# A megakernel of two decoder layers: many-head attention with scores made by query and by key, and no turned probabilities

## What is computed

```python
x = x + _L0_attn_ref(_layernorm(x), qk, ov)                  # one head, causal
x = x + _L0_xattn_ref(_layernorm(x), ctx, ctx, mask, ...)    # 16 heads of 16, masked
x = x + _L0_ffn_ref(_layernorm(x), ...)                      # top 4 of 16 blocks
x = x + _L1_attn_ref(_layernorm(x), ...)                     # 16 heads, no mask
x = x + _L1_xattn_ref(_layernorm(x), ctx, ctx, tokens, ...)  # 16 heads, rotary, masked
x = x + _L1_ffn_ref(_layernorm(x), ...)                      # 2 of 8 experts, and shared
```

```python
scores = jnp.einsum('bqhd,bkhd->bhqk', qh, kh) * scale       # masked where the stage says so
probs = jax.nn.softmax(scores, axis=-1)
out = jnp.einsum('bhqk,bkhd->bqhd', probs, vh)
```

## Time and profile before

| | us |
|---|---|
| median of 3 runs | 775.46 (774.58 to 775.52) |
| span of the profiled execution | 771.1 |
| S1, from its first scores | 136.62 |
| S3 | 147.21 |
| S4 | 160.77 |

### The profile page before, as it was taken

The page is one execution under the profiler, slowest core; times in us unless marked ns, Lnnn a source line. Parts: engine busy times, 40 slices in busy tenths (PEclk is TensorE's granted clock), DMA queues, the critical chain, the costliest instruction groups (busy, mean ns, idle before and its releaser), DMA issues.

```text
span 771.1 us, 16963 instructions
## 1 busy us (share of the span) xinstructions
PE 743.9 (96%) x5960; PEld 608.3 (79%) x5960; DVE 540.9 (70%) x1461; ACT 415.1 (54%) x1236; POOL 332.9 (43%) x461
## 2 busy tenths in 40 slices
PE   8999999999899999999999999999999999999997
PEld 7887777776688888887788787777877768878885
DVE  4666787888664543558777777778898888766645
ACT  3445677777532222237777766776666776333320
POOL 2323333434233311244222326567778855725540
PEclk9999999999999999999999999999999999999999
DMA  8903244220274555710000003000000001245538
GB/s 308 385 4 80 74 115 112 78 77 2 66 198 132 150 153 154 188 24 1 2 1 2 2 1 125 14 15 15 16 14 30 28 30 49 91 123 162 164 110 307
DMA packets 67042, 69.46 MB, mean 90 GB/s; under 512 B 22448, under 2 KB 57648, under 8 KB 65936
## 3 DMA queue, kind: packets, MB, share of 16 engines
q1 hardware_dynamic: 63552, 59.03, 25.3%
q0 software_dynamic: 3408, 9.34, 3.6%
HBM read 38.96 MB, written 29.40 MB: 89 GB/s over the span
## 4 chain that ended last, share of the span: by engine, by line
PE 66%; DVE 16%; POOL 8%; issue 6%; ACT 2%; DMA 1%; SPq 0%; POOLq 0%; DVEq 0%
PE pj L379 10%; PE pj L372 8%; PE pj L466 8%; PE ov L541 7%; PE sc L528 7%; PE sc L455 6%; POOL routed_y L1834 5%; PE ov L477 4%; DVE mx L1028 4%; PE pj L366 4%; DVE pT L1035 3%; PE sc L673 2%; PE sc L450 2%; PE ov L379 2%; ACT pr L1562 1%
## 5 line engine op out<-in xcount | busy, mean ns | idle before, releaser
L1562 ACT ACTIVATE pr<-sc,mx 128x128 f32<-128x128 f32 x768 | 216.7, 396 | 85.3 <-DVE mx L1028 83.2
L1028 DVE TENSOR_REDUCE mx<-sc 128x4 f32<-128x512 f32 x192 | 125.6, 682 | 27.1 <-PE sc L455 25.8
L466 PE MATMUL pj<-idn,pr 128*128 128x128 f32 x768 | 121.8, 283 | 7.5 <-ACT pr L1562 2.4
L466 PEld LDWEIGHTS pj<-idn,pr 128*128 128x128 f32 x768 | 84.1, 141 | 46.1 <-issue 26.1
L1035 DVE COPY pT<-pj 128x512 f32<-128x512 f32 x128 | 87.5, 685 | 22.7 <-PE pj L466 22.5
L1752 POOL TENSOR_SCALAR ve<-mv 128x2 f32<-128x2 f32 x40 | 13.7, 342 | 156.3 <-DVE mv L957 155.8
L1582 ACT ACTIVATE hT<-sc,vecs 128x256 f32<-128x256 f32 x64 | 30.3, 474 | 90.3 <-PE sc L528 90.3
L541 PE MATMUL ov<-W,hT 128*128 128x256 f32 x256 | 61.3, 382 | 1.4 <-DVE hT L1122 1.4
L528 PE MATMUL sc<-xnT,W 128*128 128x256 f32 x256 | 60.9, 381 | 0.0
L1777 POOL TENSOR_SCALAR kM<-kraw,vecs 128x256 f32<-128x256 f32 x64 | 34.5, 553 | 51.8 <-ACT kraw L1545 51.8
L1545 ACT ACTIVATE pT<-pj 128x512 f32<-128x512 f32 (+1 forms) x72 | 41.7, 589 | 28.1 <-PE pj L466 27.7
(11 more groups left out here) (229 smaller groups left out, 1509.5 us busy)
## 6 DMA issues: line engine op xcount, KB each, us to landing
sorted_x<-more_xT SPq DMA_DIRECT2D x15, 1152.0 KB, 7.4
kM<-sorted_x SPq DMA_DIRECT2D x39, 129.0 KB, 2.1
cT<-in_ctxT SPq DMA_DIRECT2D x16, 256.0 KB, 3.5
pr<-kept_at SPq DMA_DIRECT2D x32, 128.0 KB, 3.2
pT<-kept_at SPq DMA_DIRECT2D x32, 128.0 KB, 3.3
W<-in_w SPq DMA_DIRECT2D x2, 1024.0 KB, 14.1
cT<-in_ctx SPq DMA_DIRECT2D x8, 256.0 KB, 3.8
W<-in_w_gu SPq DMA_DIRECT2D x1, 2048.0 KB, 8.4
```

The source lines that it names most:

```text
L466: last = tr(bank[b][:, i * S:(i + 1) * S], pr[n % 4][:, i, :], idn[:])
L1028: v.tensor_reduce(mx[n % 4][:], four(b), AX.X, ALU.max, negate=True).then_inc(mx_done, 1)
L1562: last = a(pr[n % 4][:, i, :], bank[b][:, i * S:(i + 1) * S], ACT.Exp, bias=mx[n % 4][:, i:i + 1])
```

## The change

Scores of a many-head half are made twice. First by query (`by_query`): queries on partitions, as before, for the maxima only. This is done one half ahead (`following(U, j)`). VectorE writes the negated maxima of 16 heads side by side into `mx[j]`; TensorE turns them (`turn_maxima`), ScalarE copies them to `mxT`, and SyncE moves them by two small transfers (`shift`) into the 16 spare rows of each strip of `qM`. Then by key (`by_key`): keys on partitions. The keys `kM` have a row of ones where `qM` has the maxima, so the matmul itself subtracts them. ScalarE makes exponentials of a whole bank in one call without bias, and the result is already laid out for the product with the values: `turn_probs` and `copy_probs` are gone.

Both queries and keys are now split into even and odd heads by ScalarE (`apart`, `turned`), in calls with a scale and a shift per partition; `masked_keys` on GpSimd is gone. Each pass has 16 calls of 128 columns in place of 8 of 256. Masks are needed in both layouts: `mb0`, `mb1` by query, and new `mbT0`, `mbT1` by key, built once by VectorE from a second mask tensor and a transposed causal one. By query, banks in `DVE_MAXED` get the mask and their maxima in one VectorE operation, `tensor_tensor_reduce`, once per head; the others are loaded with the mask by TensorE. By key, banks in `DVE_MASKED` get it by `add_mask`.

Keys are made two units ahead, in S4 the rotation too. SyncE's program is written by halves, with the fills of `sorted_x` in another place: five before unit 8, two in each of units 16-20. The spread choice lands in `pr`, `oT` and `hd`.

```diff
+        DVE_MAXED = {1: (1, 2, 3, 5, 6, 7), 4: (3, 7)}
+        DVE_MASKED = {1: (3, 7), 3: (), 4: ()}
...
                 for c in range(C):
-                    for b, strip, added in sides:
-                        last = mm(bank[b][:, c * T:(c + 1) * T], qT[U % 2][strip, c, j * S:(j + 1) * S],
-                                  kM[U % 2][strip, c, j, :, :], start=not added, stop=True,
-                                  skip_group_check=True)
+                    for i in two:
+                        for b, strip, added in sides:
+                            o = (2 * c + i) * S
+                            last = mm(bank[b][:, o:o + S], qM[U % 2][strip, c, i, s], kM[U % 2][strip, c, i, s],
+                                      start=not added, stop=True, skip_group_check=True)
...
+            def turn_maxima(U, j):
+                b, n = begin("pj", "mT", U, j)
+                pe.wait_ge(drained[b], n - 1)
+                pe.wait_ge(*emptied("n", U, 4 * j + 3))
+                tr(bank[b][0:H, 0:S], mx[j][:], idn[:]).then_inc(filled[b], 1)
...
+                pe.wait_ge(s_shift[j], 32 * (att(U) + 1))
...
+                            last = mm(bank[b][:, o:o + S], kM[U % 2][strip, c, i, s], qM[U % 2][strip, c, i, s],
+                                      start=not added, stop=True, skip_group_check=True)
...
-            def turn_probs(U, n):
-                b, k = begin("pj", "pT", U, n)
-                pe.wait_ge(drained[b], k - 1)
-                pe.wait_ge(*emptied("s", U, n))
-                for i in range(4):
-                    last = tr(bank[b][:, i * S:(i + 1) * S], pr[n % 4][:, i, :], idn[:])
-                last.then_inc(filled[b], 1)
...
+                        for c in range(C):
+                            for i in two:
+                                some = bank[b][:, (2 * c + i) * S:(2 * c + i + 1) * S]
+                                last = v.tensor_tensor_reduce(some, some, side, -1.0, 3.0e38, ALU.add, ALU.min, dst[:, c, i:i + 1])
...
-                for i in range(4):
-                    last = a(pr[n % 4][:, i, :], bank[b][:, i * S:(i + 1) * S], ACT.Exp, bias=mx[n % 4][:, i:i + 1])
+                a(pr[n % 4][:], four(b), ACT.Exp).then_inc(drained[b], 1)
...
+            def shift(U, j):
+
+                sp.wait_ge(*emptied("mT", U, j))
+                for i in two:
+                    sp.dma_start(qM[U % 2][16 * (1 - i):P:32, :, i, j * S:(j + 1) * S],
+                                 mxT[j][8 * i:8 * i + 8, :]).then_inc(s_shift[j], 16)
```

More of the change, by code:

```diff
@@ L57 @@
 VEC = {}
-for _name, _n in (("bq0", C), ("bk0", C), ("b1", FF), ("bq1", C), ("bk1", C), ("gq", C), ("gk", C),
-                  ("gv", C), ("go", C), ("even", 1), ("odd", 1), ("place", B), ("lane", 1)):
+for _name, _n in (("bq0", 2 * C), ("bk0", 2 * C), ("b1", FF), ("bq1", 2 * C), ("bk1", 2 * C), ("gq", C), ("gk", C),
+                  ("gv", C), ("go", C), ("mine", 2), ("unit", 2), ("quarter", 2), ("sixteenth", 2), ("place", B),
+                  ("lane", 1)):
     VEC[_name] = (sum(n for _, n in VEC.values()), _n)
@@ L297, in attends, with masked @@
             return stage(U) in ATT
[L299 to L305, removed]
+        def masked(U, n):
+            f, p = U // PAIRS, U % PAIRS
+            here = DVE_MASKED[f]
+            return (f == 4) * PAIRS * len(DVE_MASKED[1]) + p * len(here) + sum(m <= n for m in here)
         def att(U):
@@ L434, in output0, with preload, by_query @@
                 along_tokens(b, cnT[U % 2], Wov)
-            def scores(U, j):
+            def preload(b, masks, p, j):
+                mm(bank[b][:, :], idnb[:], masks[:, 2 * p + j:2 * p + j + 1, :].to_broadcast([P, 4, S]),
+                   start=True, stop=False, skip_group_check=True)
+            def by_query(U, j):
                 f, p = U // PAIRS, U % PAIRS
@@ L1430, in alone0 @@
                     keep_hidden(U, 0)
-                if stage(U + 2) in (0, 1, 2, 3) and stage(U) not in (0, 1):
+                if stage(U + 2) in (0, 1, 2) and stage(U) not in (0, 1):
                     x_norm(U + 2)
@@ L1653, in part0 @@
                 if f == 0:
[L1654 to L1658 removed]
+                    copy_out(qT[(U + 1) % 2], "q", U + 1)
+                elif f in (1, 3):
+                    queries(U + 1, (1, 3).index(f))
+                elif f == 4:
+                    turned(qM[(U + 1) % 2], "qT", U + 1, "quarter")
                 if late(U, 35) is not None:
@@ L1769, in x_norm @@
                 last.then_inc(xn_done, 1)
-            def masked_keys(W, name, *what):
-                pool.wait_ge(*emptied(*what))
-                for o in range(C):
-                    src = kraw[:, o, :].rearrange("p (j s) -> p j s", j=2)
-                    for i, half in enumerate(("even", "odd")):
-                        shift = zero[:, 0:1] if name is None else V(name, o)
-                        last = g.tensor_scalar(kM[W % 2][:, o, :, i, :], src, shift, V(half), ALU.add, ALU.mult)
-                last.then_inc(kM_done, 1)
             def rotate(W, i):
@@ L2003, in _ @@
+            for U in range(PAIRS - 1, UNITS - 1):
+                for j in two:
+                    (part0, part1)[j](U)
+                    N = following(U, j)
+                    if attends(N[0]):
+                        shift(*N)
             for r in range(4):
```

514 lines of the change are left out of this document (240 added, 274 removed).

## The result

The changed kernel takes 802.83 us (median of 4 runs, 801.61 to 804.29) against 775.02 for the kernel before, run beside it: a ratio of 1.0366, 95% interval 1.0344 to 1.0387. The profiled execution's span is 800.3 us, 29.2 more than the 771.1 before. The forecast was +8.0, so the direction was right and the size was not.

A forecast was written before the change was run, and what follows sets the result against it. TensorE, busy 96% of 771.1 us, was taken as the bound, with the score banks as other resource. Terms 11.0 - 6.5 + 1 + .5 + 2 = +8.0 gave span 779.1, median 783.5; range 775 to 793, wide 761 to 808.

The forecast's parts named there:

- the second can make it up to about 2.5 later: +2 over the stage, between 0 and 4: Units 16 to 20: a second blank fill ahead of the kept-block hand-over delays it; +2 us, between 0 and 4.
- S1, +11.0: Many-head stage, units 8-15: the bank loop makes a half 9.18 us against 8.49, sixteen times .69.
- 3.51, the forecast's figure: From the start of key-side scores to the next query-side ones: pass, exponentials and hand-overs, 3.51 us.
- 5.67: S1, from query-side to key-side scores: pass, plain reduction, 12 pairs, tail and hand-over on the banks, 5.67 us.
- the pair: VectorE's add-and-reduce plus accumulator read for S1 maxima, four per bank: .31 us each, between .27 and .46.
- TensorE's 5.14: S1, from query-side to key-side scores: TensorE's own work, 5.14 us, the floor even with free pairs.
- rival B: Faster, chance 0.30: pairs hide behind TensorE's 5.14, S1 +2.6; 765 us, 760 to 773; decided by a pair below .27.
- rival C: Pairs in S1 do not overlap: .46 each, 1.80 us more per half, +29: 812 us; chance 0.13.
- S3 and S4, -6.5 and +1: Units 24-31: less TensorE work, -6.5 us over eight units; units 32-39: more mask preloads, +1 us.
- the bank wait of .48: Half 1 of each S3 unit: the banks need 3.51 us, TensorE has 3.03 of work, costing .48.
- rival E: Small transfers of maxima land late: each microsecond beyond 8 comes once per half, 48 times; 800 to 830 us; chance 0.05.
- rival D: Weight loads set the pace of a score pass: 1.5 instead of 1.15 in 96 passes, +34: 817 us; chance 0.06.

The follow-up runs named there:

- e1: Changed kernel with one blank fill ahead of the hand-over in each of units 16 to 23, the last two in units 24 and 25: 780.26 us, ratio 1.0087.
- e3: Kernel before with only the changed kernel's fill placement (five at the start, two per unit in units 16 to 20): 789.44 us, ratio 1.0199.
- e8: e4 with S1's value projection moved to a unit's first half and pairs taken from one bank: 780.11 us, ratio 1.0092.
- e7: e4 with the 12 pairs of each S1 half replaced by three plain reductions, masks left out of these maxima: 774.05 us in a single run.
- e4: Changed kernel without fills in units 16 to 23: seven moved to units 7 to 13, three to units 24 to 26: 775.17 us, ratio 1.0026.
- e11: Changed kernel with the two fills of units 16 to 20 issued by GpSimd at the unit's start instead of SyncE: 808.39 us in a single run.
- e9: e4 with two masks per S4 half moved from TensorE to VectorE: 773.69 us, ratio .9993.
- e2: Changed kernel with the two fills of units 16 to 20 issued behind the kept-block hand-over and its reads: 793.34 us, ratio 1.0269.

## Why the prediction was right or wrong

**Wrong, and it is the miss: "the second can make it up to about 2.5 later: +2 over the stage, between 0 and 4".** This term measured 23.2 us (e1 against after), and 15.7 when nearly the same was done to the kernel before (e3). I took a fill's landing, 7.4, as a delay to be partly covered, and priced the hand-over once. Two things were missing. A hidden fill says nothing about a second: in the kernel before, one fill had nearly drained before the write was wanted (none or one, 148.3 and 148.2), so the first cost nothing, and the second had no cover left. And SyncE works in order and waits for the landing of the write before it issues the reads (fills, write, reads, next fills), so each unit pays for the whole lengthening.

The price was in reach, from landings and issues put behind one another in SyncE's order. Behind the write come the issues of eight reads and a context, in the kernel before:

```profile
233.64 5.13 SPq L1982 DMA_DIRECT2D pr<-kept_at  x8
238.82 0.59 SPq L1990 DMA_DIRECT2D cT<-in_ctx  x1
```

My estimate from these rows: one fill's 7.4, the write's 1.7 and these 5.7 make 14.8, less than the period of 16.7, so one fill is hidden; two fills, 14.8, and these 5.7 make 20.5 even without the write, and the measured period is 20.6 (14.5 of it from the first fill's issue to the write's landing). The 155 GB/s of the window before would not have told it: they are what one fill per unit asked for, and the engines moved 199 while two fills drained.

That the changed kernel lost 23.2 and the one before 15.7 lies for the larger part in unit 16, whose fills e3 issued in S1. Its block reads start at 217.26 in after and at 211.94 in e1, 5.3 earlier; they start at 203.75 in e3 and at 204.45 before. The rest, some 2 us, stays open.

**S1, +11.0: too high.** Up to S1 and S1 together grew by 3.7 us, and 1.6 of that is one half at a low clock. TensorE's rows of two clean halves:

```profile
121.96 1.17 PE L471 MATMUL sc<-kM,qM 32*128 32x128 f32 x32
...
127.08 1.17 PE L500 MATMUL sc<-qM,kM 32*128 32x128 f32 x32
128.18 0.28 PE L480 MATMUL pj<-idn,mx 128*16 128x128 f32 x1
129.01 0.38 PE L448 MATMUL sc<-mb,idnb 128*128 128x512 bf16 x1 [0.55 <-ACT pr L1542]
130.59 1.17 PE L471 MATMUL sc<-kM,qM 32*128 32x128 f32 x32 [1.20 <-ACT pr L1542]
```

From key-side scores to the next query-side ones it is 3.51, the forecast's figure, with the holes ended by ScalarE where they were said to be. In the other half of a unit it is 3.69, filled by the key projection. A pass is 1.17 (1.15). From query-side to key-side scores it is 5.12, where I had 5.67: the mis-sized term is the pair. VectorE's rows in that stretch:

```profile
123.31 0.68 DVE L1051 TENSOR_REDUCE mx<-sc 128x4 f32<-128x512 f32 x1
123.91 0.29 DVE L1049 CUSTOM_DVE_ANT_0 sc<-sc,mb 128x128 f32<-128x128 f32 x1
124.12 0.14 DVE L1049 DVE_READ_ACCUMULATOR2_ANT mx<- 128x1 f32 x1
124.12 0.33 DVE L1049 CUSTOM_DVE_ANT_0 sc<-sc,mb 128x128 f32<-128x128 f32 x1
124.36 0.14 DVE L1049 DVE_READ_ACCUMULATOR2_ANT mx<- 128x1 f32 x1
124.36 0.33 DVE L1049 CUSTOM_DVE_ANT_0 sc<-sc,mb 128x128 f32<-128x128 f32 x1
...
126.85 0.14 DVE L1049 DVE_READ_ACCUMULATOR2_ANT mx<- 128x1 f32 x1
```

A pair takes .25, not .31, under even my lower bound of .27, since the read of the accumulator lies wholly beside the next operation. So TensorE's 5.14, which I had worked out as the floor, decides, by .19 (e8), and without pairs nothing is gained (e7). That is rival B's S1, and B's point of decision, a pair under .27, was met. The Trainium skill, "VectorE: DVE Perf Modes", section "The DRAIN you can't avoid", says that the next operation waits until the pipeline is empty, but also that one that is not held starts earlier; the prediction drew on the first sentence alone. Operations .33 long that start .25 apart agree with the second, and rival C is out.

**S3 and S4, -6.5 and +1: together right, apart not.** They measured -1.1 and -4.5, -5.6 in all against -5.5. The steady S3 unit is as forecast: 16.91 us instead of 17.54, -.63 where I had -.82, with the bank wait of .48 seen as .40:

```profile
418.00 1.17 PE L500 MATMUL sc<-qM,kM 32*128 32x128 f32 x32
...
421.50 1.17 PE L471 MATMUL sc<-kM,qM 32*128 32x128 f32 x32 [0.40 <-ACT pr L1542]
```

Its last four halves, in which S4's first projections are made ahead, took 2 us back. S4 fell although I counted nothing for the copies that VectorE lost there.

**The rest.** Behind S4 3.7 us were lost; this part lies between 128.1 and 132.4 over the runs of the changed kernel and its variants, and between 127.9 and 129.4 over the kernel before and its two, so these runs don't tell how much of it, if any, the change costs. The waits for the small transfers never show on TensorE (rival E), and weight loads do not set the pace (pass 1.17, rival D). The sum of the forecast without the fills, +6.0, stands beside the +2.0 of e4's span.

## What to carry to other kernels

Before moving a bulk transfer into a stretch that has one already, walk through the issuing engine's program for one period: put the landings that it has to wait behind, one after another, and its issue times, and compare the sum with the period. A transfer that is hidden says nothing of a second one. A small transfer on which a loop turns is late by what the transfer engines hold when it comes. Moving the bulk to another queue did not help here; moving it to a stretch without such a loop did. And read slack only from a stretch at the full granted clock.

## What the runs showed of the hardware

- A 16 KB write landed 1.4 us after its issue in seven of the eight units of e4, where no fill stands near it, 6.5 to 7.7 close behind 2.3 MB of fills (after), and up to 11.9 behind fills from another queue (e11).
- An issue is not always short: a second 1152 KB fill held SyncE for 3.66 us, and the 9 KB one behind it for 2.99, where the first took .43 and .66.
- VectorE's add-and-reduce of 128x128 with its accumulator read goes every .25 us; the read (.14) lies beside the next operation (.33).
- TensorE's granted clock fell in steady halves of S1 from 2.4 to 1.2 GHz for some microseconds in after, e1, e4, e7 and e9 (the window of .54 above is nearly all at the lower level), and not in e2 and e11, whose code in S1 is that of after. It fell behind a hole of 1.75 us, as every second half there has one; the half in which it did lasts 10.42 in after instead of 8.82.
